# A selective scan with a mixture of experts in one loop: expert steps as single weight slices dealt to the pairs by a running sum, and the convolution off VectorE

## The reference, cut to what matters

```python
xn = layernorm(x)                                   # x: 4096 tokens x 256, fp32
# branch 1: a selective scan over 4096 steps, 128 channels x 64 states
y = layernorm(xn) * gamma + beta
left, right = split(y @ W_up + b_up)                # 128 columns each
left = silu(causal_conv(left, conv_w, 3 taps) + conv_b)
delta = softplus(left @ W_delta + b_delta); B = left @ W_B; C = left @ W_C
h[t] = exp(delta[t] * A) * h[t-1] + delta[t] * left[t] * B[t]
s = xn + ((sum over states of h[t] * C[t] + left[t] * D) * silu(right)) @ W_down + b_down
# branch 2: 8 experts, every token goes to its best two
g = silu(sum over the two of weight * (silu(xn @ w1[e]) * (xn @ w3[e])) @ w2[e])   # 256 -> 1024 -> 256
out = x + s * g
```

## Time and profile before

| | |
|---|---|
| median of 3 runs | 1383.98 us (1377.9 to 1392.47) |
| the profiled execution's own time | 1385.34 us |
| its span, first to last instruction | 1382.9 us |
| main loop, first to last scan | starts 117.3 to 1341.5 us, 512 pairs |
| granted TensorE clock, mean over the span | 0.933 |

### The profile page before, as it was taken

One profiled execution on the slowest core, in us unless ns is written; L12 is line 12 of the kernel. 1 busy time (PEld: TensorE's weight loads), 2 busy tenths in 40 slices (PEclk: granted clock), 3 DMA queues, 4 the chain that ended last, 5 costly groups with the idle time before them and its releaser, 6 DMA issues.

```text
span 1382.9 us, 26003 instructions
## 1 busy us (share of the span) xinstructions
PE 1205.3 (87%) x7688; PEld 938.9 (68%) x7688; DVE 1193.4 (86%) x1634; ACT 734.1 (53%) x1583; POOL 1089.5 (79%) x1048
## 2 busy tenths in 40 slices
PE   4846788999999999998899989998999999989761
PEld 4725366877677777876687768686777777877530
DVE  6747588999799998989798979898989988988988
ACT  1361556555655565546554565456545565545642
POOL 0346278898899788888998788788979788988994
PEclk8579999999999999999999999999999999999655
DMA  7111264646364645564556436643664457464458
GB/s 211 61 39 46 67 212 135 168 141 214 110 175 143 198 148 165 147 212 121 148 147 211 126 119 180 214 142 103 172 211 139 127 155 230 143 222 149 144 175 291
DMA packets 124316, 216.51 MB, mean 157 GB/s; under 512 B 15040, under 2 KB 40768, under 8 KB 124160
## 3 DMA queue, kind: packets, MB, share of 16 engines
q10 hardware_dynamic: 73728, 134.25, 33.9%
q1 hardware_dynamic: 43616, 61.83, 13.6%
q0 software_dynamic: 6816, 18.62, 4.2%
HBM read 190.67 MB, written 23.99 MB: 155 GB/s over the span
## 4 chain that ended last, share of the span: by engine, by line
PE 68%; POOL 9%; issue 8%; DVE 6%; DMA 4%; ACT 3%; SPq 1%; ACTq 0%; DVEq 0%; POOLq 0%
PE bank L1222 31%; PE bank L1192 14%; PE bank L1170 8%; PE bank L1236 6%; POOL arena L433 4%; DMA wring<-in_w_all 3%; PE bank L1099 2%; POOL hid L448 2%; DVE arena L964 2%; PE bank L1115 1%; PE bank L1135 1%; PE bank L1068 1%; PE bank L1061 1%; SPq L386 1%; PE bank L1205 1%
## 5 line engine op out<-in xcount | busy, mean ns | idle before, releaser
L433 POOL TENSOR_TENSOR arena<-arena,c_rep 128x512 f32<-128x512 f32 x512 | 607.1, 1190 | 153.4 <-DVE arena L964 145.6
L964 DVE TENSOR_TENSOR_SCAN arena<-bank,carry,arena 128x512 f32<-128x512 f32 x512 | 652.5, 1275 | 30.7 <-ACT bank L733 30.5
L1222 PEld LDWEIGHTS bank<-xgT,wring 128*128 128x128 f32 x4288 | 518.3, 194 | 138.4 <-issue 99.3
L1222 PE MATMUL bank<-xgT,wring 128*128 128x128 f32 x4288 | 540.6, 280 | 50.5 <-issue 26.4
L733 ACT ACTIVATE bank<-arena,a_neg 128x512 f32<-128x512 f32 x512 | 354.2, 692 | 107.7 <-ACT bank L733 43.2
L955 DVE TENSOR_TENSOR arena<-bank,b_rep 128x512 f32<-128x512 f32 x512 | 351.8, 687 | 42.6 <-PE bank L1236 23.4
L662 ACT ACTIVATE th<-bank 128x256 f32<-128x256 f32 x284 | 108.9, 383 | 347.0 <-PE bank L1222 324.9
L1236 PE MATMUL bank<-stack,pick 128*128 128x512 f32 x512 | 279.1, 546 | 8.3 <-DVE arena L955 7.9
L1192 PE MATMUL bank<-wring,hid 128*128 128x256 f32 x1072 | 271.4, 386 | 8.2 <-POOL hid L448 7.4
L1192 PEld LDWEIGHTS bank<-wring,hid 128*128 128x128 f32 x1072 | 196.1, 191 | 64.4 <-issue 24.6
L448 POOL TENSOR_TENSOR hid<-gt,ue 128x256 f32<-128x256 f32 x284 | 209.6, 738 | 15.4 <-DVE gt L976 11.8
(11 more groups left out here) (172 smaller groups left out, 818.9 us busy)
## 6 DMA issues: line engine op xcount, KB each, us to landing
arena<-delta_d ACTq DMA_DIRECT2D x512, 256.0 KB
wring<-in_w_all SPq DMA_DIRECT2D x64, 384.0 KB, 5.6
xn<-in_x SPq DMA_DIRECT2D x4, 1024.0 KB, 9.9
xn_d<-xn SPq DMA_DIRECT2D x4, 1024.0 KB, 5.5
parts_d<-spare SPq DMA_DIRECT2D x16, 256.0 KB
stack<-parts_d SPq DMA_DIRECT2D x16, 256.0 KB, 5.7
wring<-results SPq DMA_DIRECT2D x8, 512.0 KB, 7.3
arena<-results SPq DMA_DIRECT2D x8, 512.0 KB, 7.9
```

The costliest lines, as they stand in the source:

```text
L433: pool.tensor_tensor(p_ring[:, s % P_RING, :], h_ring[:, s % H_RING, :], of_chunk(c_rep, c, 2), ALU.mult).then_inc(s_hc, 1)
L964: v.tensor_tensor_scan(out=h_ring[:, s % H_RING, :], data0=a_bank[s % 2][:, :], data1=b_ring[:, s % B_RING, :], initial=carry[:, q:q + 1], ...
L1222: ins = pe.matmul(bank[:, m * SW + r * SLOT:m * SW + (r + 1) * SLOT], wring[:, 2 * j + r, (2 * m + h) * P:(2 * m + h + 1) * P], xgT[:, i % ...
```

## The change

Four things change.

- The turn `step` is split: `half` multiplies the first slice of a step and `step` the second, in the same bank, each with its own wait for its slice. The elementwise work after a step is unchanged.
- `turns_by_pair` no longer uses a table. `expert_turns` writes one list in a fixed order, and the turns are dealt to pairs by a running sum of costs over 490 pairs from pair 16: each pair is charged 0.34, every fourth 0.97 more for the sums over states, a half and a step 0.9 each, an out 0.86, rows 0.44, a guest 0.86, and the turns of tiles from 68 on 0.65 of that. Guests stand at one place in a tile, between its last `half` and `step`, once they are due.
- The banks are fixed: step j uses bank j mod 2, and `rows` and all guests use bank 0. So `rows` waits for VectorE's read of step 0, `half` 2 waits for the eviction of the next tile's `rows`, a guest waits for the read of step 2, and `half` 0 of the next tile waits until the guest has been read.
- For chunks 1 to 7 the taps are three products on ScalarE (pairs 11 to 13) and two sums on GpSimd (13 and 14). The two tanhs and the two additions of 1 are dealt to pairs of their own (16 to 19), the two products on GpSimd to 20 and 21.

```diff
+def expert_turns():
+    def turn(kind, n):
+        return [(kind, n // STEPS, n % STEPS)] if 0 <= n < STEPS * TILES else []
+    items = [("rows", 0, 0)]
+    for n in range(STEPS * TILES + 3):
+        i, j = n // STEPS, n % STEPS
+        items += turn("half", n)
+        if j == 1 and i + 1 < TILES:
+            items.append(("rows", i + 1, 0))
+        if j == 3:
+            items.append(("guest", i, 0))
+        items += turn("step", n) + turn("out", n - 2)
+    return items
...
+    for s in window:
+        used += fixed[s]
+        while at < len(items) and used + cost(items[at]) / 2 <= rate * (s - MOE_FIRST + 1):
...
+            def add_taps(c, part):
+                pool.wait_ge(s_taps, 3 * (c - 1) + part + 2)
+                if part:
+                    pool.wait_ge(s_first_sum, c)
+                pool.tensor_tensor(stage("cv"), stage("cv"), stage(("thl", "thr")[part]), ALU.add
+                                   ).then_inc(s_cvs if part else s_first_sum, 1)
...
+            def tap_product(c, part):
+                if part == 0:
+                    act.wait_ge(s_partd, STORES * c)
+                    act.wait_ge(s_lrev, c + 1)
+                tap = 2 - part
+                act.activation(stage(("cv", "thl", "thr")[part]), of_chunk(c_rep, c, tap), ACT.Identity,
+                               bias=0.0 if part else half[:, 3:4], scale=half[:, tap:tap + 1]).then_inc(s_taps, 1)
...
-            def gate_and_up(i, j):
+            def gate_and_up(i, j, r):
+                bank, k = bank_of(("step", i, j)), 2 * j + r
...
-                for k in (2 * j, 2 * j + 1):
-                    pe.wait_ge(s_w[k], 16 * (i + 1))
+                pe.wait_ge(s_w[k], 16 * (i + 1))
...
+                kind, i, j = turn
+                n = STEPS * i + j
+                if kind == "half":
+                    ge(pe, s_gt, n - 1)
+                    if j == 2 and i + 1 < TILES:
+                        pe.wait_ge(s_xgT, i + 2)
+                    elif j == 0 and GUEST_OF[i]:
+                        guest_gone(*GUEST_OF[i])
+                elif kind == "rows":
+                    pe.wait_ge(s_lrev, NC)
+                    ge(pe, s_gt, STEPS * (i - 1) + 1)
```

More of the change, by code:

```diff
@@ L38 @@
 PLACED_AT = 6
[L39 to L44, removed]
+MOE_PAIRS = 490
+LIKELY = FULL + E // 2
+SPREAD, REDUCE = 0.34, 0.97
+COST = dict(half=0.9, step=0.9, out=0.86, rows=0.44, down=0.86, delta=0.86, b=0.86, c=0.86)
+WORK_AFTER = dict(conv=("pairs", 11), add=("pairs", 13), tanh=("pairs", 16), sigmoid=("pairs", 18), silu=("pairs", 20),
+                  right=("pairs", 21),
                   exp=("delta", 2), ln=("delta", 3),
@@ L47 @@
                   stack=("delta", 17))
-WORK_PARTS = dict(sum=4, conv=3)
+WORK_PARTS = dict(sum=4, conv=3, add=2, tanh=2, sigmoid=2)
 BIAS_AT = 61
-def turns_by_pair():
[L54 to L80, removed]
@@ new lines, in cost @@
+def cost(turn):
+    return COST.get(turn[0], 0) * (0.65 if turn[1] >= LIKELY and turn[0] in ("half", "step", "out", "rows") else 1)
+def turns_by_pair():
+    by_pair, before = [[] for _ in range(PAIR_COUNT + 1)], {}
+    items, due = expert_turns(), guests_by_pair()
+    fixed = [SPREAD + (REDUCE if s % 4 == 3 else 0) for s in range(PAIR_COUNT)]
+    window = range(MOE_FIRST, MOE_FIRST + MOE_PAIRS)
+    rate = (sum(cost(t) for t in items) + sum(cost(t) for s, t in due) + sum(fixed[s] for s in window)) / MOE_PAIRS
+    used, at, guest = 0.0, 0, None
+    for s in window:
+        used += fixed[s]
+        while at < len(items) and used + cost(items[at]) / 2 <= rate * (s - MOE_FIRST + 1):
+            kind, i, j = turn = items[at]
+            at += 1
+            if kind == "guest":
+                if not due or due[0][0] > s:
+                    continue
+                turn = guest = due.pop(0)[1]
+            if kind == "half" and j == 0:
+                before[i], guest = guest, None
+            by_pair[s].append(turn)
+            used += cost(turn)
+    assert at == len(items) and not due
@@ L250, in bank_of @@
         def bank_of(turn):
-            return gu_bank[NUMBER[turn] % 2]
+            kind, i, j = turn
+            if kind == "step":
+                return gu_bank[j % 2]
+            return gu_bank[j if kind == "down" and i == NC - 1 else 0]
         def product_bank(c, kind):
@@ L706, in _ @@
             evict_conv(0)
-            tanhs(0)
-            sigmoids(0)
+            for part in range(2):
+                tanhs(0, part)
+            for part in range(2):
+                sigmoids(0, part)
             scale_rows(3)
@@ L983, in gate_chunk @@
                 v.tensor_tensor(sr[:, c % 2, :], y_bank[:, :], sr[:, c % 2, :], ALU.mult).then_inc(s_gated, 1)
[L985 to L995, removed]
             def add_rows(c, h):
```

121 lines of the change are left out of this document (67 added, 54 removed).

## The result

The changed kernel takes 1392.85 us (median of 20 runs, 1382.54 to 1400.33), the kernel before 1383.33 us (20 runs, 1377.9 to 1392.47). The ratio is 1.0065 with a 95% interval of 1.0045 to 1.0084: slower by 0.65%, where 1.7% faster was forecast. It lies inside the wide range of 1338 to 1398, outside the forecast's own 1345 to 1376, and on the wrong side of the kernel before.

A forecast was written before the change was run, and what follows sets the result against it. TensorE and VectorE were taken as saturated together. Terms -20 -11 -3 -3 +3 +2 +6 +3 = -23 us from the profiled 1385.3 give 1362, predicted as 1361 for the median; own range 1345 to 1376, wide range 1338 to 1398.

The forecast's parts named there:

- Weights, +6: At changes of expert, slots are needed sooner after their out: stalls of 2.3 us a change, +6 us taken (+2 to +37).
- The rival of late weights: All weight loads land like four in a row; long stalls and TensorE's slower clock give 1408 us; chance 0.17.
- Dealing, -11: Turns dealt by cost over pairs 32 to 479 leave fewer overlong TensorE pairs: 11 us gained (1 to 39).
- the 3 + 3 us that I booked for softplus and outs' waits: More work before `rows`' first user around a softplus, and more room for outs awaiting GpSimd: 3 us gained each.
- the +2 for banks: Fixed banks make `rows` and `half` 0 wait for reads, mostly covered: 2 us lost (0 to 10).
- The second rival: No gain from dealing, as TensorE evens it out or has room: 1372 us, chance 0.14.
- both ends keep their work: The last 40 pairs (dead tiles) and both ends of the kernel keep their work; no term was given.
- Convolution, -20 + 3 for GpSimd: Taking 21 tap instructions off VectorE gains 20 us (8 to 27); two sums a chunk on GpSimd cost 3 in all.
- third rival: GpSimd becomes the bound between pairs 13 and 38, costing 18 us in place of 3: 1376 us, chance 0.13.
- The sign named beforehand: Waits on the gate ahead of `rows`, held to be covered, would show the forecast wrong; no size given.
- Loads of x, +3: SyncE's eight loads of x at pair 460 delay a slot: a wait of about 7 us, 3 us lost.
- the pace of 2.09 in quiet stretches: Scans start 2.09 us a pair in undisturbed stretches, taken to show that TensorE's peaks are mostly evened out already.

The follow-up runs named there:

- the two versions: Changed kernel with the first `rows` turn at pair 15: 1389.02 us; changed kernel with both slices in turn `step` for tiles from 64 on: 1390.97 us.
- The two kernels with one load: Kernel before with only the convolution moved, and the changed kernel, each loading expert weights for the first tile only: 1353.99 and 1354.08 us.
- a second trace with the same turns: Trace of the changed kernel with both slices of a step in turn `step` for tiles from 64 on, so no added branch: 1390.97 us.

## Why the prediction was wrong, step by step

- **Weights, +6: the step that failed.** The reloads cost 39 us instead of 12, so the term was +27, within its bounds of 2 to 37 but far from the value taken. The landing times were not the mistake, as far as they are known: the trace has them for 24 of the 64 loads, 5.6 us in the median and 4.5 to 7.2, and for none of the last four of a change. Three other things were. I let each stall give the next slice its room and came to 2.3 us a change; the waits are 25.4 / 7 = 3.6, and 4.1 to 4.3 in the two versions. I priced a stall at its own length; with the reloads TensorE's busy time in the long stretch grew by 19 us (13 and 8 in the versions) where it had grown by 4 before. And a guest in the same pair holds VectorE's queue, so the scans lose the rest as well. How the +27 divides between the three is not shown, as no run takes away one of them alone. The rival of late weights had this mechanism, and its condition, "once a change of expert costs over 5 us", was met (39 / 7 = 5.6), with loads that landed earlier than it supposed. Its price of 16 us for the clock is matched by the profiled execution (19 - 4 = 15) but not by the versions (9 and 4), so that match is luck. Its time of 1408 was too high.
- **Dealing, -11 (bounds 1 to 39): mis-sized, measured 0, give or take some 7.** The two kernels with one load are equal, 1354.0 and 1354.1. This takes in the 3 + 3 us that I booked for softplus and outs' waits and the +2 for banks. The second rival, that TensorE evens it out, holds for the sum. The pair table, with the reloads, splits it: 3.2 us in ordinary pairs and 1.8 around the softplus came, and start and tail took 5.5 each. Both of these I had left out: "both ends keep their work" was true of the work and not of its order.
- **Convolution, -20 + 3 for GpSimd: right mechanism, right size without reloads.** -16 with one load, -10 with them. The 6 us between (reloads cost 18 with the convolution moved and 12 without) are not clear of the noise of these medians, and from scan 32 to scan 480 the traces give 18 in both cases. The three distances up to scans 14, 15 and 16 of a chunk, where the taps stood, fall from 3.25 us in the mean to 2.27 with the convolution alone, 20 us over 21 distances; other pairs take part of it back. GpSimd as the bound (third rival) did not come: with the convolution alone TensorE waited 7.9 us for `hidden` products (7.4 before) and 6.5 for the states times C (7.6 before). The Trainium skill (GPSIMD Engine Reference, Engine selection) puts elementwise sums on VectorE because GpSimd is about half as fast. The price agrees, 1.271 against 0.72 us, but the move wins here, where VectorE is nearer to its limit than GpSimd (86% against 79% busy before).
- **Bank waits, +2 ("mostly covered"): too low.** The sign named beforehand, waits ahead of `rows`, is there in the changed kernel with 12.5 us in 12 waits, and with 12.4 us where nothing is reloaded; before it was 2.0 in 2. So these waits are about 10 us more, part of the dealing's 0. There is no margin either: with `rows` 0.9 us nearer to step 0 they became 43.5 us.
- **Loads of x, +3:** 2.7 us in the pair table, a wait of 6.28 where 7 was foreseen.
- **What bounds the kernel.** TensorE and VectorE together, as said: giving work away from VectorE paid, evening TensorE out gave nothing in sum. This fits TensorE's mean, and not its peaks, being what counted, as the pace of 2.09 in quiet stretches had said. It isn't proved: the dealing may have won in the ordinary pairs what its bank waits, start and tail took back.

With the sizes measured, -16 + 0 + 27 = +11 is the difference of the medians in the table. The three steps lead from one end of that table to the other, so they must add up to it, and the sum is no check of the causes.

## What to carry to other kernels

When an order is changed to even out an engine, count the slack of every reload (last use to next use) first, and price a stall on a saturated engine with what may follow it: the slower clock, in some executions, and the queue behind. An engine that already keeps its best pace in quiet stretches may have little to win from an even deal. Before trusting a split edit, run its parts alone, and once with the transfers taken out: here such runs told which part won and which lost. And before a cause is read off one trace, look at a second execution of the same order.

## What the hardware showed that I had not expected

- A wait of 2.6 us of TensorE was followed by 3 us at a granted clock of 0.55. All seven changes of expert of the changed kernel's trace show a mean of 0.93 to 0.96 over 24 us, but only two of seven before, whose waits were at most 2.4 us, and only two of seven in a second trace with the same turns, where waits of 2.27 and 2.33 us had no fall behind them and one of 2.69 had.
- Eight matmuls of 128x128 took 1.82 us in that stretch against 0.89 outside it. TensorE's total busy time with reloads was 1220.4 us, and 1200.3 with the same instructions and one load. Busy time holds the time at the lower clock, so two kernels' busy times can be compared only with the granted clock beside them.
